# A fused attention and two-layer block on Trainium2: scores of heads 0 to 3 in the turning banks, with all orders redrawn

## The reference

```
def _layer(x, ...):
    q, k, v = split(shift_token(x) @ wqkv)               # 8 heads of 64
    q, k = rotary_xpos(l2norm(q) * qs, l2norm(k) * ksc)
    sim  = einsum('bhwid,bhwjd->bhwij', q * 8, k)        # window of 128 rows, 256 keys
    attn = softmax(where(mask, -max, sim))
    o    = einsum('bhwij,bhwjd->bhwid', attn, v)
    x    = x + o @ wo
    h    = layernorm(shift_token(x)) @ w1 + b1
    a, g = split(h)
    return x + (a * gelu(g)) @ w2 + b2
```

## Time and profile before

| | us |
|---|---|
| median of 3 runs | 2610.24 |
| lowest and highest run | 2607.21, 2612.92 |
| the profiled execution | 2607.61 |
| span of its instructions | 2605.8 |
| PE busy | 2554.4 |
| DVE, ACT, POOL busy | 2200.3, 2048.0, 1692.2 |

### The profile page before, as it was taken

How to read it: one execution, slowest core, us unless ns; L and a number is a source line. 1 busy time by engine, 2 the same in 40 slices (tenths; PEclk the granted TensorE clock), 3 DMA queues, 4 the chain that set the end, 5 groups by cost and what they waited for, 6 DMA issues and landing times.

```text
span 2605.8 us, 65082 instructions
## 1 busy us (share of the span) xinstructions
PE 2554.4 (98%) x21792; PEld 2259.0 (87%) x21792; DVE 2200.3 (84%) x6610; ACT 2048.0 (79%) x5140; POOL 1692.2 (65%) x1850
## 2 busy tenths in 40 slices
PE   8899999999999999999999999999999999999997
PEld 5677788888999989999899998898988898889896
DVE  4778987888888888888888889898998889998885
ACT  5665788788888888888888888888788887888784
POOL 5533864666666666666666677777777767776673
PEclk9999999999999999999999999999999999999999
DMA  9853411111122111111113321122211222112120
GB/s 296 272 166 102 132 38 41 39 48 32 44 59 63 42 38 38 46 44 45 39 33 94 114 54 43 39 54 54 54 43 41 53 54 54 40 42 56 48 54 23
DMA packets 164990, 173.91 MB, mean 67 GB/s; under 512 B 20120, under 2 KB 130224, under 8 KB 163888
## 3 DMA queue, kind: packets, MB, share of 16 engines
q1 hardware_dynamic: 164656, 169.76, 22.6%
HBM read 80.02 MB, written 51.92 MB: 51 GB/s over the span
## 4 chain that ended last, share of the span: by engine, by line
PE 87%; ACT 3%; DVE 3%; issue 2%; DMA 2%; POOL 1%; SPq 1%; DVEq 0%; ACTq 0%; POOLq 0%
PE p_pair L158 17%; PE p_pair L159 14%; PE p_pair L160 14%; PE p_values L2708 8%; PE p_mixed L158 5%; PE p_mixed L160 5%; PE p_mixed L159 5%; PE p_turn L2689 4%; PE p_turn L2664 2%; PE p_turn L2670 2%; PE p_turn L2696 2%; PE p_mixed L2725 1%; PE p_values L518 1%; PE p_mixed L2634 1%; PE p_turn L476 1%
## 5 line engine op out<-in xcount | busy, mean ns | idle before, releaser
L1051 POOL TENSOR_TENSOR inv_norm<-norm_clipped,minus_half 128x8 f32<-128x8 f32 x256 | 441.8, 1726 | 259.9 <-DVE norm_clipped L1876 259.5
L1350 ACT ACTIVATE prob<-prob,least 128x256 f32<-128x256 f32 (+1 forms) x1024 | 495.5, 485 | 21.5 <-DVE least L1912 13.2
L1912 DVE CUSTOM_DVE_ANT_0 prob<-p_pair,mask,inv_norm 128x256 f32<-128x256 f32 (+1 forms) x1024 | 435.1, 460 | 45.3 <-PE p_pair L160 40.5
L158 PE MATMUL p_pair<-hT_h,w_h 128*128 128x256 f32 (+1 forms) x1408 | 412.1, 293 | 3.3 <-DVE hT_l L1971 2.5
L159 PE MATMUL p_pair<-hT_l,w_h 128*128 128x256 f32 (+1 forms) x1408 | 394.8, 280 | 0.0
L160 PE MATMUL p_pair<-hT_h,w_l 128*128 128x256 f32 (+1 forms) x1408 | 394.7, 280 | 0.0
L158 PEld LDWEIGHTS p_pair<-hT_h,w_h 128*128 128x128 f32 (+1 forms) x1408 | 264.2, 188 | 11.6 <-DVE hT_l L1971 2.7
L1085 POOL TENSOR_TENSOR mixed<-prob 128x256 f32<-128x256 f32 x224 | 165.9, 741 | 152.2 <-DVE rinv L1920 87.3
L160 PEld LDWEIGHTS p_pair<-hT_h,w_l 128*128 128x128 f32 (+1 forms) x1408 | 264.7, 188 | 0.0
L1981 DVE SCALAR_TENSOR_TENSOR gated<-p_pair,columns,gelu 128x256 f32<-128x256 f32 (+1 forms) x384 | 181.6, 479 | 97.2 <-ACT gelu L1407 89.7
L159 PEld LDWEIGHTS p_pair<-hT_l,w_h 128*128 128x128 f32 (+1 forms) x1408 | 263.5, 187 | 0.0
(11 more groups left out here) (157 smaller groups left out, 8770.4 us busy)
## 6 DMA issues: line engine op xcount, KB each, us to landing
v_prev_first<-v_own_first SPq DMA_DIRECT2D x256, 128.0 KB, 2.3
x_tile<-x_rows SPq DMA_DIRECT2D x192, 128.0 KB, 2.2
a_wraw<-in_w_all SPq DMA_DIRECT2D x32, 264.0 KB, 4.3
w_high<-a_wraw_h SPq DMA_DIRECT2D x32, 264.0 KB, 3.5
w_low<-a_wraw_l SPq DMA_DIRECT2D x32, 264.0 KB, 4.4
...
x_tile<-x_rows SPq DMA_DIRECT2D x128, 64.0 KB, 2.0
```

The costliest lines, as they stand in the source:

```text
L158: pe.matmul(out, lh, rh, start=start, stop=False)
L1051: pool.tensor_tensor(r[:, t.slot(2), heads], rt[:, heads], half[:, heads], ALU.pow).then_inc(pool_r[n], 1)
L1350: act.activation(prob[:, h, cols], prob[:, h, cols], ACT.Exp, bias=least[:, h:h + 1], scale=-1.0, accum_out=rsum[:, h:h + 1]).then_inc(act ...
L1912: dve.tensor_tensor_reduce(prob[:, h, cols], p_score[h % 2][:, c0 + cols.start:c0 + cols.stop], mask[:, a.slot(2), cols], r[:, a.slot(2), ...
```

## The change

`scores` of group 0 writes `p_turn` instead of `p_score`, and `least_of` reads heads 0 to 3 from there. Group 1 stays where it was. With two sets of banks both groups can be written before either is read. The lists of all five engines are drawn anew, ahead of the steps, in the step and behind the steps. Counted over the whole program, the runs of consecutive `scores` products fall from 255 to 130, and ACT_TABLE_LOADs rise from 132 to 246; all other work is the same.

```diff
-                dve.tensor_tensor_reduce(prob[:, h, cols], p_score[h % 2][:, c0 + cols.start:c0 + cols.stop],
+                bank = (p_score if group else p_turn)[h % 2]
+                dve.tensor_tensor_reduce(prob[:, h, cols], bank[:, c0 + cols.start:c0 + cols.stop],
...
-                ins = three_pass(pe, p_score[h % 2][:, c0 + cols.start:c0 + cols.stop],
+                bank = (p_score if group else p_turn)[h % 2]
+                ins = three_pass(pe, bank[:, c0 + cols.start:c0 + cols.stop],
                                  (qT_h[rows, m], qT_l[rows, m]), (kh, kl), True, True)
...
         @block.tensor
...
-            all_steps(t.step, 12, 60)
+            all_steps(t.step, 11, 60)
```

More of the change, by code:

```diff
@@ L1523, in last_steps @@
             gated_high(Q(112), 5)
+            exponential(T(116), 3)
+            k_high(T(117))
+            q_high(T(117))
+            exponential(T(116), 4)
             exponential(T(116), 5)
             exponential(T(116), 6)
+            exponential(T(116), 7)
             squares(T(118), 1)
-            exponential(T(116), 7)
+            squares(T(118), 0)
+            probs_out(T(116), 0)
+            probs_out(T(116), 1)
+            mixed_out(T(116))
+            x_high(T(119))
+            v_out(T(118))
             exponential(T(117), 0)
@@ L1572, in last_steps @@
             gated_high(Q(114), 5)
+            exponential(T(118), 3)
+            k_high(T(119))
+            q_high(T(119))
+            exponential(T(118), 4)
             exponential(T(118), 5)
@@ L1604, in last_steps @@
             o_high(T(119))
+            gelu(Q(116), 4)
+            gelu(Q(116), 5)
+            gated_high(Q(116), 3)
+            gated_high(Q(116), 4)
+            gated_high(Q(116), 5)
+            k_high(T(121))
+            q_high(T(121))
             exponential(T(120), 3)
@@ L1719, in last_steps @@
             gated_high(Q(120), 5)
+            k_high(T(125))
+            exponential(T(124), 3)
+            q_high(T(125))
+            exponential(T(124), 4)
             exponential(T(124), 5)
@@ L4334, in first_on_scalar @@
     t.exponential(T(0), 3)
-    t.x_high(T(2))
+    t.v_out(T(1))
+    t.k_high(T(1))
     t.q_high(T(1))
@@ L4386, in first_on_scalar @@
     t.exponential(T(3), 3)
-    t.x_high(T(5))
-    t.v_out(T(4))
     t.exponential(T(3), 4)
@@ L4429, in first_on_scalar @@
     t.exponential(T(5), 4)
-    t.gelu(Q(0), 3)
-    t.gated_high(Q(0), 2)
-    t.q_high(T(6))
-    t.gelu(Q(0), 4)
-    t.gelu(Q(0), 5)
-    t.gated_high(Q(0), 3)
-    t.gated_high(Q(0), 4)
-    t.gated_high(Q(0), 5)
-    t.k_high(T(6))
-    t.o_high(T(4))
-    t.x_high(T(7))
     t.exponential(T(5), 5)
@@ L4443, in first_on_scalar @@
     t.exponential(T(5), 7)
+    t.gelu(Q(0), 3)
+    t.o_high(T(4))
+    t.gelu(Q(0), 4)
+    t.gelu(Q(0), 5)
+    t.k_high(T(6))
+    t.gated_high(Q(0), 3)
+    t.gated_high(Q(0), 4)
+    t.q_high(T(6))
+    t.gated_high(Q(0), 5)
+    t.x_high(T(7))
+    t.probs_out(T(5), 0)
+    t.probs_out(T(5), 1)
+    t.mixed_out(T(5))
     t.v_out(T(6))
     t.exponential(T(6), 0)
+    t.squares(T(7), 1)
     t.exponential(T(6), 1)
@@ L4539, in first_on_scalar @@
     t.exponential(T(9), 7)
+    t.gated_high(Q(4), 0)
+    t.o_high(T(8))
+    t.gelu(Q(4), 2)
+    t.gelu(Q(4), 3)
+    t.x_high(T(11))
+    t.gated_high(Q(4), 1)
+    t.gated_high(Q(4), 2)
+    t.gelu(Q(4), 4)
+    t.gelu(Q(4), 5)
+    t.k_high(T(10))
+    t.gated_high(Q(4), 3)
     t.gated_high(Q(4), 4)
-    t.k_high(T(10))
     t.gated_high(Q(4), 5)
+    t.q_high(T(10))
     t.squares(T(11), 0)
+    t.probs_out(T(9), 0)
+    t.v_out(T(11))
     t.h_high(Q(6))
-    t.v_out(T(11))
+    t.exponential(T(10), 0)
+    t.exponential(T(10), 1)
+    t.x_high(T(12))
     t.squares(T(11), 1)
-    t.probs_out(T(9), 0)
     t.probs_out(T(9), 1)
     t.mixed_out(T(9))
-    t.x_high(T(12))
-    t.q_high(T(11))
-    t.exponential(T(10), 0)
-    t.exponential(T(10), 1)
     t.exponential(T(10), 2)
@@ L6511, in first_on_tensor @@
     t.project_v(T(3))
-    t.after((signal.dve_least, T(2), H, 4))
+    t.after((signal.act_pT, T(1), 3, 3))
+    t.scores(T(2), 0)
     t.scores(T(2), 1)
-    t.after((signal.act_pT, T(1), 3, 3))
+    t.turn_x(T(4))
     t.values(T(1), 0)
@@ L6646, in first_on_tensor @@
     t.values(T(5), 2)
+    t.after((signal.pool_p, T(6), 3, 1))
+    t.turn_probs(T(6), 0)
+    t.after((signal.dve_hv, Q(2), 1, 1))
+    t.output(T(4))
+    t.project_v(T(7))
     t.values(T(5), 3)
@@ L6649, in first_on_tensor @@
     t.turn_q(T(7))
-    t.after((signal.dve_kr, T(7), 1, 1))
-    t.project_v(T(7))
-    t.turn_probs(T(6), 0)
-    t.turn_x(T(8))
+    t.after((signal.pool_k, T(7), 1, 1))
+    t.after((signal.act_pT, T(6), 3, 1))
+    t.turn_k(T(7))
     t.after((signal.dve_hT, Q(2), 1, 1))
@@ L6711, in first_on_tensor @@
     t.widen(Q(2), 5)
-    t.after((signal.dve_kT, T(8), 1, 1))
-    t.turn_mixed(T(7))
-    t.turn_q(T(9))
+    t.after((signal.act_pT, T(7), 3, 3))
     t.scores(T(8), 0)
-    t.turn_x(T(10))
-    t.after((signal.act_pT, T(7), 3, 3))
+    t.scores(T(8), 1)
     t.values(T(7), 0)
@@ L6741, in first_on_tensor @@
     t.project_v(T(10))
+    t.after((signal.act_pT, T(8), 3, 1))
+    t.after((signal.pool_p, T(8), 3, 3))
+    t.turn_mixed(T(8))
     t.after((signal.dve_x, T(2), 1, 1))
     t.output(T(7))
+    t.after((signal.act_pT, T(8), 3, 3))
+    t.scores(T(9), 0)
+    t.scores(T(9), 1)
     t.after((signal.act_v, T(10), 1, 1))
@@ L6911, in first_on_tensor @@
     t.turn_x(T(15))
-    t.scores(T(13), 1)
-    t.after((signal.act_pT, T(12), 3, 3))
     t.values(T(12), 0)
@@ L6938, in first_on_tensor @@
     t.turn_mixed(T(13))
+    t.after((signal.dve_gt, Q(10), HF + 1, 1))
+    t.widen(Q(10), 2)
+    t.after((signal.act_pT, T(13), 3, 3))
     t.scores(T(14), 0)
-    t.after((signal.act_pT, T(13), 3, 3))
+    t.scores(T(14), 1)
     t.values(T(13), 0)
```

5113 lines of the change are left out of this document (2450 added, 2663 removed).

## The result

The changed kernel takes 2637.71 us (median of 4 runs, 2635.35 to 2638.87) beside 2610.16 us of the kernel before on the same chip: ratio 1.0105, 95% interval 1.0087 to 1.0122. It is slower by 27.5 us; the forecast was 10 us slower (2620), with a range from 2591 to 2645. Its profiled execution took 2636.92 us, 29.3 more than that of before.

The account below looks back on a forecast made before the run. PE's issue bounded the kernel before; afterwards ACT's chain would set full steps. Repeated steps -1.8 + 9.5 + 5.4 = +13 us, -3 outside, total +10: 2617.6 profiled, 2620 us median, range 2591 to 2645.

Parts of the forecast that it names:

- Rival 3: DVE ends late in the second layer, delaying `widen` 0 by 0.5 to 1 us; 2632 to 2660; 0.13 together with Rival 5.
- Rival 5: Joined scores save nothing on PE; forecast rises by 20 to 2640; 0.13 together with Rival 3.
- the chain over ACT's two `mixed_out`: From `turn_mixed(T(5))` to the next step's scores: 21.05 us, 0.9 longer than PE's 20.15 us of work beside it.
- Rival 1: ACT keeps up and the saving stands: full step 35.9 to 36.1 us, total 2584 to 2602; chance 0.26.
- rival 2: Chain only 0.3 to 0.5 us longer than PE's work, waits eat the saving: 2602 to 2612; chance 0.17.
- the saving on PE: Joined scores and fewer borders, less added re-entries, shorten PE's work by 0.45 us a step.
- The term for reading other banks: `least_of` on DVE reads one PSUM bank as before, so reading other banks costs nothing.
- the second layer: Same ACT chain, DVE with 10% left: 18 full steps at 37.0 to 37.1 us, +0.3 each, +5.4 in all.
- the full steps of the first layer: ACT's chain sets 19 steps in the repeated list: 36.9 us each, +0.5, together +9.5 us.
- Steps with a first tile: Twelve steps of the repeated list, shorter chain, PE sets them: gain 0.15 us each, -1.8 in all.
- outside the repeated list: Some 13 redrawn steps' worth: PE can win up to 6 us or lose as much; taken as -3.
- Rival 4: Each table switch stops ACT about another 1.28 us beyond the load: 96 us more, about 2716; chance 0.02.

Follow-up runs that it names:

- e1: Changed kernel with GELU replaced by an exponential, so 246 table loads become 1 (numbers not the reference's): 2607.59 us, ratio 0.9991.
- e15: e13 with GELU replaced by an exponential, so ACT loads a table once (numbers not the reference's): 2593.58 us, ratio 0.9938.
- e2: Kernel before the change with GELU replaced by an exponential, 132 table loads become 1 (numbers not the reference's): 2603.45 us, ratio 0.9973.
- e12: Changed kernel, odd tiles' score banks swapped, mixed heads normalised, turned and copied first at the step's end for the even tile: 2627.70 us, ratio 1.0077.
- e13: e12 with the second layer's `final` calls moved behind `gated` 1 of the next step, two stores after tile 113's load: 2616.08 us, ratio 1.0026.
- e14: Changed kernel with `final` calls moved behind `gated` 1 of the next step and two stores placed after tile 113's load: 2636.55 us, ratio 1.0107.

## Why the prediction was right or wrong, point by point

**The time is in the range, but not by the forecast's own path.** 2637.71 lies outside the 2612 to 2632 given to the forecast and inside the 2632 to 2660 of rivals 3 and 5, which had 0.13. That the range from 2591 to 2645 holds it is owed to its reach into those rivals; as far as the forecast's own sum goes, it is luck. The loss is nearly three times the one forecast; the points below say which terms were right and which were not.

**Right: the bound and its successor.** PE set the step before, and the successor was named: the chain over ACT's two `mixed_out`, with three loads in it. Measured 21.17 us for 21.05, and 15.05 for 15.0 of it on ACT; the full step 36.95 for 36.9. An addition of 30 pieces held to 0.1 us because ACT had no pause in it, so that only durations had to be summed. Rival 1 (the saving stands) and rival 2 (nothing to measure) failed by this; with the loads gone (e1) the step is 36.16, which is nearly its 36.1.

**Slightly too large: the saving on PE.** Forecast 0.45 a step. The joint itself is as forecast (24 scores in 1.61 us). Between two kernels without loads, e15 and e2, a full step differs by 0.3; between after without loads (e1) and e2 by 0.14. The term for reading other banks, put at nothing, holds: in after `least_of` takes 0.48 us from `p_turn` and from `p_pair`.

**Mis-sized, and the main error: the second layer.** Forecast +0.3 in 18 full steps and -0.15 in six with a first tile, 4.5 us; measured +16.1 from pair 34 to 56. The term assumed that ACT's chain alone could hold PE, and took DVE's 10% of free time as a margin. Rival 3 had the mechanism, `widen` 0 released by `q_rot` because DVE's list ends late, but held it for a separate case that adds 0.5 to 1 us to each step at a chance of 0.13. It is there, together with the forecast's own chain: the 11.6 us beyond the forecast are 0.53 for each of 22 steps. It is worst where I did not look, in the step behind a first tile: 38.4 where before has 36.6 to 37.1. That DVE's crowded end costs this is shown for 11.4 us by e12 and e13, which differ only in the finals and their stores: 811.3 against 799.9. That its share is small while POOL's product is late (e14, 4.2) fits two waits in a row. Why DVE comes so late behind a first tile's step, even in e1 and e13, no run separates.

**Too small: the full steps of the first layer behind a first tile.** Their distance is 37.13 to 37.34, where I had taken 36.9 for all full steps; what they have beyond the others is PE's wait for `q_rot` of 0.2 to 0.36, again DVE. The first layer's part of the repeated list lost 14.0 instead of 8.6 us: 2.1 in its first step, 4.9 here, and 7.7 in the 14 other full steps (0.55 each for a forecast of 0.5). Steps with a first tile gain 0.12 in the first layer, forecast 0.15; in the second they lose 0.25.

**Too hopeful by 2 us: outside the repeated list.** Forecast -3; measured +3.0 - 6.7 + 2.7 + 0.2 = -0.8. The -6.7 between pairs 0 and 7 is the gain of which I thought; the start varies by as much as it weighs.

**Right: the price of a switch.** Rival 4 is excluded by the rows, in which nothing stands beside the load, and its 2716 by the time. Rival 5, that the joined scores are worth nothing, falls by the 0.12 at the joint and by e15.

**What stays open.** e13 without its loads is at 36.0, with them at 36.40; which of the four loads makes these 0.4 I did not separate. Nor is it settled why DVE is late behind a first tile's step in every kernel of the new order.
